# A planned eight-image kernel: quarter mask products, array halves, packed denominators, one spreading load

## Time and profile before

| what | value |
|---|---|
| median of 3 runs | 984.56 us (983.65 to 985.37) |
| span of the profiled execution, first to last instruction | 980.1 us |
| busy: PE, DVE, ACT, POOL | 875.3, 595.7, 457.1, 204.5 us |
| mean granted clock of PE | 0.962 of full speed |

### The profile page before, as it was taken

How to read it: one execution, slowest core, us unless ns; L and a number is a source line. 1 busy time by engine, 2 the same in 40 slices (tenths; PEclk the granted TensorE clock), 3 DMA queues, 4 the chain that set the end, 5 groups by cost and what they waited for, 6 DMA issues and landing times.

```text
span 980.1 us, 22296 instructions
## 1 busy us (share of the span) xinstructions
PE 875.3 (89%) x9216; PEld 588.9 (60%) x9216; DVE 595.7 (61%) x1666; ACT 457.1 (47%) x764; POOL 204.5 (21%) x274
## 2 busy tenths in 40 slices
PE   9888798999999999999999999999988879978876
PEld 8675475566666665666566566656555555644553
DVE  5545534673688468845884588558844764653456
ACT  1003326453555355525543655356435645524754
POOL 1002100120225012401341124112411231131122
PEclk9999689999999999999999999999979999998988
DMA  7100000000000000000000001000100100030000
GB/s 198 25 7 1 1 6 23 23 23 28 23 23 23 28 23 23 23 28 23 23 23 28 7 23 39 23 1 23 39 11 26 36 23 23 23 81 23 2 1 22
DMA packets 25572, 25.84 MB, mean 26 GB/s; under 512 B 14688, under 2 KB 20576, under 8 KB 25344
## 3 DMA queue, kind: packets, MB, share of 16 engines
q1 hardware_dynamic: 25472, 24.42, 8.7%
HBM read 19.69 MB, written 4.72 MB: 25 GB/s over the span
## 4 chain that ended last, share of the span: by engine, by line
PE 58%; DVE 17%; ACT 11%; issue 6%; DMA 5%; POOL 2%; SPq 1%; POOLq 0%; DVEq 0%; ACTq 0%
PE ring L934 7%; PE pv L955 5%; PE side_a L633 5%; PE ring L889 5%; PE pv L973 4%; ACT pr L1190 4%; DVE rden L1676 3%; DMA scale<-branch_scale 3%; PE heads L879 2%; PE side_a L642 2%; PE heads L914 2%; PE ring L929 2%; DMA branch_scale<-rden 2%; PE heads L861 2%; PE ring L897 2%
## 5 line engine op out<-in xcount | busy, mean ns | idle before, releaser
L1190 ACT ACTIVATE pr<-ring 128x1024 f32<-128x1024 f32 (+1 forms) x128 | 120.9, 944 | 108.3 <-PE ring L938 61.0
L934 PE MATMUL ring<-kq 64*128 64x256 f32 (+2 forms) x1280 | 136.5, 341 | 0.7 <-ACT kq L1242 0.5
L934 PEld LDWEIGHTS ring<-kq 64*128 64x128 f32 x1280 | 96.3, 191 | 42.6 <-issue 30.8
L1234 ACT ACTIVATE kq<-ring 128x896 f32<-128x896 f32 x64 | 58.8, 919 | 85.3 <-PE ring L889 85.3
L1686 DVE SCALAR_TENSOR_TENSOR ob<-pv,all_gates,scale 128x256 f32<-128x256 f32 x96 | 46.3, 482 | 85.3 <-PE pv L973 38.4
L1661 DVE TENSOR_REDUCE toks<-heads 128x2 f32<-128x512 f32 x64 | 44.3, 692 | 84.8 <-PE heads L919 83.4
L573 POOL TENSOR_TENSOR toks<-ta,tb 128x128 f32<-128x128 f32 (+1 forms) x96 | 39.7, 434 | 180.4 <-DVE tb L1652 180.4
L1242 ACT ACTIVATE kq<-ring 128x256 f32<-128x256 f32 x64 | 24.6, 384 | 107.5 <-PE ring L897 107.0
L1676 DVE RECIPROCAL rden<-pv 128x256 f32<-128x256 f32 x32 | 56.2, 1756 | 25.5 <-PE pv L955 25.0
L536 POOL TENSOR_TENSOR oT<-ob 128x256 f32<-128x256 f32 x32 | 23.3, 727 | 226.3 <-DVE ob L1686 226.3
L889 PE MATMUL ring<-early,toks 128*128 128x128 f32 x448 | 63.5, 284 | 7.5 <-ACT pr L1190 7.4
(11 more groups left out here) (377 smaller groups left out, 1704.4 us busy)
## 6 DMA issues: line engine op xcount, KB each, us to landing
scale<-branch_scale SPq DMA_DIRECT2D x128, 96.0 KB, 2.3
branch_scale<-rden SPq DMA_DIRECT2D x32, 128.0 KB, 1.7
late<-in_late SPq DMA_DIRECT2D x1, 2158.5 KB, 8.4
xin<-in_x SPq DMA_DIRECT2D x16, 64.0 KB, 2.2
pr<-in_prep SPq DMA_DIRECT2D x1, 602.0 KB, 3.8
y<-ob SPq DMA_DIRECT2D x8, 64.0 KB, 1.9
kq<-in_masks SPq DMA_DIRECT2D x1, 480.0 KB, 8.5
toks<-in_final SPq DMA_DIRECT2D x1, 434.0 KB, 4.4
```

The costliest lines, as they stand in the source:

```text
L934: m = pe.matmul(ring[:, j, at:at + nq], kq[rows, k, key0:key0 + P], kq[rows, k, Q + q_:Q + q_ + nq], start=r % 2 == 0, stop=at > P)
L1190: act.activation(out, in_, ACT.Exp, scale=SCALE).then_inc(S("exp_done"), 1)
L1234: act.activation(kq[:, k, :], flat[:, 0:WIDE], ACT.Copy).then_inc(S("turned"), 1)
```

## The change

- **Quarter masks.** The mask products run on quarters: for each head (half of the rows) and each half of the output partitions one product of a 64x64 block of the identity with 64 partitions of the table. The blocks off the diagonal need the tables with their partition halves exchanged: `crossed`, loaded by two more DMAs and cast on DVE.
- **3x3 convolution.** Each tap becomes two products of 128 columns, one per half image, on the two column halves. The sum with the input then stands in 128 partitions: two DVE additions, and one transpose instead of two.
- **Experts, q and keys/values.** `xp` is written twice side by side by DVE, so that one transpose gives `xpT` in both partition halves. The four hidden products use a half of the rows each (64 partitions) and all stand behind `logit_exp`; ScalarE waits once for all of them. Keys and values use the upper half, q the lower. Two more DMAs put the second halves of `w1` and of `q3` at partitions 64 to 127.
- **Denominators.** Row `32j + 2 br + x` holds branch `br` and token half `x`: six rows of 128 columns instead of three of 256. 32 products instead of 24, a reciprocal of 128 x 128, a store of half the bytes, and one load for all four heads.

```diff
-        onesk = sb("onesk", [P, BR, 32])
+        onesk = sb("onesk", [P, BR, 2, 32])
...
+            sp.dma_start(crossed32[0:C, :], masks_in[C:P, P:mn]).then_inc(S("masks"), 16)
+            sp.dma_start(crossed32[C:P, :], masks_in[0:C, P:mn]).then_inc(S("masks"), 16)
...
+            sp.dma_start(late[C:P, a:a + 2 * P], late_in[0:C, a:a + 2 * P]).then_inc(S("head_weights"), 16)
+            sp.dma_start(late[C:P, q:q + P], late_in[0:C, q:q + P]).then_inc(S("head_weights"), 16)
...
-                    for j in range(4):
-                        sp.dma_start(scale[32 * j:32 * j + 32, :, :], scale_out[32 * j:32 * j + BR, :].unsqueeze(0)
-                                     .broadcast_to((32, BR, T))).then_inc(S("scale_loaded"), 16)
+                    sp.dma_start(scale[:, :, :].rearrange("p b t -> p (b t)"),
+                                 scale_out.rearrange("(j r) t -> j (r t)", j=4)[:, 0:BR * T].unsqueeze(1)
+                                 .broadcast_to((4, 32, BR * T))).then_inc(S("scale_loaded"), 16)
...
                 for i, (copy, dy, dx) in enumerate(PAIRS3):
-                    m = pe.matmul(SA[0:C, 0:T], bin1[:, i, :], window(copy, dy + 1, dx + 1), start=(i == 0),
-                                  stop=(i == 4))
+                    for up in range(2):
+                        m = pe.matmul(SA[C * up:C * up + C, 0:P], bin1[:, i, :], half_window(up, copy, dy + 1, dx + 1),
+                                      start=(i == 0), stop=(i == 4))
...
-                for t in range(NT):
-                    m = pe.transpose(SA[:, t * C:(t + 1) * C], x1[0:C, t * P:(t + 1) * P], ident[0:C, 0:C])
-                m.then_inc(S("x2_turned"), 1)
+                pe.transpose(SA[:, 0:P], x1[:, 0:P], ident).then_inc(S("x2_turned"), 1)
...
-                for i in range(2):
-                    m = pe.matmul(SC[:, i * T:(i + 1) * T], w1[:, i, :], xpT[:, :], start=True, stop=True)
-                m.then_inc(S("hidden"), 1)
                 yield
                 pe.wait_ge(S("logit_exp"), image * 2 + 2)
                 for i in range(2):
-                    m = pe.matmul(SB_[:, i * T:(i + 1) * T], w1[:, 2 + i, :], xpT[:, :], start=True, stop=True)
+                    for x in range(2):
+                        rows = slice(C * x, C * x + C)
+                        m = pe.matmul((SC, SB_)[x][:, i * T:(i + 1) * T], w1[rows, 2 * x + i, :], xpT[rows, :],
+                                      start=True, stop=True)
...
-                pe.matmul(SC[:, 0:T], cst("q3"), xpT[:, :], start=True, stop=True).then_inc(S("q3_out"), 1)
-                for t in range(NT):
-                    m = pe.matmul(SB_[:, t * T:(t + 1) * T], xpT[:, t * P:(t + 1) * P], cst("kv3"),
+                for t in range(NT):
+                    m = pe.matmul(SB_[:, t * T:(t + 1) * T], xpT[0:C, t * P:(t + 1) * P], cst("kv3")[0:C, :],
                                   start=True, stop=True)
+                    if t == 0:
+                        pe.matmul(SC[:, 0:T], cst("q3")[C:P, :], xpT[C:P, :], start=True, stop=True)\
+                            .then_inc(S("q3_out"), 1)
...
-                    pe.wait_ge(S("head_weights"), 16 * 28)
+                    pe.wait_ge(S("head_weights"), 16 * 30)
...
+            def masked(banks, at, n, straight, over, first):
+
+                for j in range(2):
+                    rows = slice(C * j, C * j + C)
+                    for c in range(2):
+                        m = pe.matmul(banks[C * c:C * c + C, j, at:at + n], identb[rows, rows],
+                                      (straight if c == j else over)[rows, 0:n], start=first, stop=not first)
+                return m
...
-                    for j in range(2):
-                        pe.matmul(heads[:, j, 0:2 * P + BAND], identb, max_b, start=True, stop=False)
+                    masked(heads, 0, 2 * P + BAND, max_b, max_x, True)
...
-                    for j in range(2):
-                        m = pe.matmul(ring[:, j, 0:P], identb, score_b[:, 0:P], start=False, stop=True)
+                    m = masked(ring, 0, P, score_b, score_x, False)
...
-                pieces = [(0, 0, T, 0, 0), (0, P, T, 1, 0), (1, 0, T, 0, T),
-                          (2, P, T, 1, P), (2, P, BAND, 1, 3 * P), (2, 0, P, 1, 2 * P)]
-                for i, (br, q_, end, part, a) in enumerate(pieces):
+                pieces = [(0, 0, P, 0, 0), (0, 1, P, 0, P), (0, 1, P, 1, 0), (1, 0, P, 0, T), (1, 1, P, 0, T + P),
+                          (2, 1, P, 1, P), (2, 1, WINDOW, 1, 3 * P), (2, 0, P, 1, 2 * P)]
+                for i, (br, x, n, part, a) in enumerate(pieces):
                     for j in range(4):
-                        m = pe.matmul(PV[32 * j:32 * j + 32, T + q_:T + end], onesk[:, br, :],
-                                      prob(g, j, part, a, end - q_), start=(i == 0), stop=(i == 5))
+                        m = pe.matmul(PV[32 * j:32 * j + 32, T:T + n], onesk[:, br, x, :],
+                                      prob(g, j, part, a, n), start=(i == 0), stop=(i == 7))
...
+                act.wait_ge(S("hidden"), image + 1)
                 for u in range(2):
-                    act.wait_ge(S("hidden"), image * 2 + u + 1)
...
+                    if which in (2, 3):
+                        from_ = from_.unsqueeze(1).broadcast_to((P, 2, C))
...
-                V.tensor_tensor(x1[0:C, :], SA[0:C, 0:T], x1[0:C, :], ALU.add).then_inc(S("x2"), 1)
+                for up in range(2):
+                    rows = slice(C * up, C * up + C)
+                    a = V.tensor_tensor(x1[rows, 0:P], SA[rows, 0:P], x1[rows, up * P:up * P + P], ALU.add)
+                a.then_inc(S("x2"), 1)
...
-            dve.wait_ge(S("masks"), 16)
-            link(V.tensor_copy(masks[:, :], masks32))
+            dve.wait_ge(S("masks"), 48)
+            V.tensor_copy(masks[:, :], masks32)
+            link(V.tensor_copy(crossed[:, :], crossed32))
...
-                V.reciprocal(rden[:, :], PV[:, T:2 * T]).then_inc(S("inverted"), 1)
+                V.reciprocal(rden[:, :], PV[:, T:T + P]).then_inc(S("inverted"), 1)
```

More of the change, by code:

```diff
@@ L124, in build @@
         score_b = masks[:, P + 2 * P + BAND:P + 4 * P + 2 * BAND]
+        crossed = sb("crossed", [P, mn - P], BF16)
+        crossed32 = kq[:, :, :].rearrange("p k n -> p (k n)")[:, mn + T:2 * mn + T - P]
+        max_x, score_x = crossed[:, 0:2 * P + BAND], crossed[:, 2 * P + BAND:4 * P + 2 * BAND]
         w_sm = sb("w_sm", [P, 84])
@@ L138, in build @@
         bin1 = sb("bin1", [P, 5, C])
-        binn = sb("binn", [P, 5, C])
         bnc = sb("bnc", [P, 4])
         half = sb("half", [P, 1])
-        onesk = sb("onesk", [P, BR, 32])
+        onesk = sb("onesk", [P, BR, 2, 32])
         meank = sb("meank", [P, P])
@@ L182, in build @@
         selH = sb("selH", [P, KEEP])
-        xp = sb("xp", [P, NT, C])
+        xp = sb("xp", [P, NT, 2, C])
         xpT = sb("xpT", [P, T])
@@ L197, in build @@
         scaled_q = pr[0:C, 0, 1, 0:26 * C].rearrange("p (n c) -> p n c", n=26)
-        rden = sb("rden", [P, T])
+        rden = sb("rden", [P, P])
         scale = sb("scale", [P, BR, T])
-        scale_out = nc.dram_tensor("branch_scale", (P, T), F32, kind="Internal").ap()
+        scale_out = nc.dram_tensor("branch_scale", (P, P), F32, kind="Internal").ap()
         ob = sb("ob", [P, 2, BR, T])
@@ L209, in build @@
         hm = sb("hm", [P, 4, T])
+        binn = hm[:, :, :].rearrange("p g t -> p (g t)")[:, 0:5 * C].rearrange("p (n m) -> p n m", n=5)
         cmp_, cmq_ = keep5[:, 0:NT, :], keep5[:, NT:2 * NT, :]
@@ L449, in _ @@
             sp.dma_start(late[C:P, v:v + HEADS * VDIM], late_in[0:C, v:v + HEADS * VDIM]).then_inc(S("head_weights"), 16)
+            a, q = lo["w1"][0] + 2 * P, lo["q3"][0]
+            sp.dma_start(late[C:P, a:a + 2 * P], late_in[0:C, a:a + 2 * P]).then_inc(S("head_weights"), 16)
+            sp.dma_start(late[C:P, q:q + P], late_in[0:C, q:q + P]).then_inc(S("head_weights"), 16)
             for x in range(2):
@@ L598, in transpose_tok, with turn_twice @@
                 m.then_inc(S(done), 1)
+            def turn_twice(done):
+                pe.sem_inc(S("pe_gap"), 1)
+                for t in range(NT):
+                    m = pe.transpose(SB_[:, t * P:(t + 1) * P], xp[:, t, :, :].rearrange("p x c -> p (x c)"), ident)
+                m.then_inc(S(done), 1)
             IDLE = dict(loads=24, route1=4, route2=12,
@@ L744, in back @@
                 after(n, "xn2")
-                transpose_tok(xp, SB_, 0, "xn2_turned")
+                turn_twice("xn2_turned")
                 yield
@@ L917, in max_scores @@
                 if kind == "A":
-                    for j in range(2):
-                        m = pe.matmul(heads[:, j, P:2 * P], identb, max_b[:, 0:P], start=False, stop=True)
+                    m = masked(heads, P, P, max_b, max_x, False)
                 m.then_inc(S("max_scores"), 1)
@@ L927, in scores @@
                 else:
-                    for j in range(2):
```

(23 more changed lines are left out.)

2 lines of the change are left out of this document (1 added, 1 removed).

## The result

The change made the kernel slower: 1075.11 us median (1074.38 to 1080.62) against 984.96 before, a ratio of 1.0906 with a 95% interval of 1.0837 to 1.0975. The prediction said 944 us (926 to 968). Medians here are over all runs of a kernel, so that 984.96 holds a fourth run of 997.79 us, while the ratios leave out runs more than 1.5% above the kernel's fastest (among the experiments one run of e3 and two of e6).

The account below looks back on a forecast made before the run. PE was taken to bound the kernel, busy 89% of 980.1 us. Terms summed to 45.9 us, less 5 for first and last images and short covers: 939 us of span, 944 us median, range 926 to 968.

Parts of the forecast that it names:

- the new one lies between 2.3 and 3.8, I take 3.0: Denominators: the one load of the scale, 384 KB, was to take 3.0 us, where the old took 3.58 from last issue.
- 8.3 us become about 5.9: Denominators: reciprocal, store, issues and load of the scale together were to shorten from 8.3 us to about 5.9.
- 4.4 + 7.3: Gain from the shorter denominator chain: 4.4 us in PE's wait at L633, 7.3 at L790 together with the tail.
- PE weighs a round later, so most of it is DVE's time: Denominators: most of the shortening from 8.3 to about 5.9 us was DVE's time; PE uses the scale a round later.
- The quarters: Mask products as four 64x64 quarters at once: scores 15.0 us and maxima 9.3 saved, less 8.0 for array shape changes.
- rival 1: Mask products: quarters pair up but four do not run together, 24.3 us of the sum go, 968 us; chance 0.10.
- rival 4: Mask products: quarters run one after another, 0.72 us a group of 416 columns instead of 0.36, 1017 us; chance 0.04.
- Convolution: 3x3 convolution on column halves: 9.4 us saved over 8 images, less 1.0 for its x2 turn.
- Experts and q3: Experts' hidden products on row halves save 6.9 us; q3 running beside keys and values saves 2.6.
- Rival 2: Exp and copies, not PE, set the rounds; savings become waits before L889, L897 and L929, 962 us; chance 0.15.
- Rival 3: Mask products: every border between array shapes drains PE, 7 us more, 951 us; chance 0.12.
- PE's waits grow by more than 15 us: One of three signs named beforehand that would show the prediction wrong: PE's waits growing by over 15 us.

Follow-up runs that it names:

- e3: Changed kernel with four spreading loads, one per head, and the mask products whole again (128x128, two per group): 957.5 us, ratio 0.9709 to before.
- e6: Changed kernel with four spreading loads and the denominators as before (three rows of 256 columns a head): 977.43 us, ratio 0.9905 to before.
- e1: Changed kernel with its one spreading load cut into four, one per head, 32 partitions each: 946.84 us, ratio 0.9635 to before.
- e9: Changed kernel with four full-width loads, SP waiting for each of the first two to land before issuing the next: 1070.1 us, ratio 1.0848 to before.
- e13: Changed kernel with every denominator row given four times, so the one load reads 16 rows by 8 partitions: 947.17 us, ratio 0.9614 to before.
- e14: As e13, but one 16-row load per branch, each with its own semaphore; a branch waits for its own load alone: 942.38 us, ratio 0.9582 to before.
- e11: As e4 (three loads by branch, outermost dimension 4), but each branch waits for its own load alone: 958.55 us, ratio 0.9721 to before.
- e4: Changed kernel with the one load cut into three by branch, outermost dimension still 4, DVE waiting for all three: 1082.16 us, ratio 1.1024 to before.
- e10: Changed kernel with four stores writing each head's rows four times, and one load from 16 rows by 8 partitions: 1082.91 us, ratio 1.0971 to before.
- e2: Kernel before with only its four loads replaced by the one spreading load (three rows of 256 columns per head): 1097.52 us, ratio 1.1178 to before.

## Why the prediction was wrong

**The first step that failed** is a term: "Against it stands a load of 602 KB that landed in 3.8; the new one lies between 2.3 and 3.8, I take 3.0." It landed in 7.2 to 7.3 where the chain shows it, with a median of 6.8 over the 32 groups. The bound came from a load by bytes, and that load's outermost dimension is 128 partitions; the new one's is four. Four of 16 engines move 384 KB in 5.0 us, 16 in 2.0. By the prediction's own sum, "8.3 us become about 5.9", the chain should have shortened by 2.4 us; its median grew by 2.2, from 7.1 to 9.3. The 3.58 us that the sum took from the earlier trace rows for the old load are also a late group's: the median from the last issue to the landing is 2.3 us before, so there was less to win than 2.4.

**The second is the price of a late chain.** The prediction had counted the chain only as it gave time back, in two waits of PE and the tail (4.4 + 7.3): 11.7 us for 2.4 us of chain, some 4.9 us for each. At that price a chain 2.2 us longer would have taken the forecast from 944 to 966 us, inside its range. The step behind it, "PE weighs a round later, so most of it is DVE's time", does not hold: in 27 of the 32 groups DVE starts the first branch within 0.5 us of the landing, in the kernel before as in e1, e6, e9, e13 and after, so it stood waiting for the load nearly every time, and what PE needs stood behind it. From the start of the reciprocal to the landing, the median of the 32 groups of a trace, against the time:

| kernel | chain us | median us | clock (profiled run) |
|---|---|---|---|
| three loads, 16 rows, first third (e14) | 5.1 | 942.38 | 0.967 |
| four loads (e1) | 6.2 | 946.84 | 0.962 |
| one load, 16 rows (e13) | 6.3 | 947.17 | 0.960 |
| three loads, three waits, first third (e11) | 6.7 | 958.55 | 0.954 |
| wide denominators (e6) | 7.05 | 977.43 | 0.959 |
| before | 7.1 | 984.96 | 0.962 |
| in turn (e9) | 9.3 | 1070.1 | 0.882 |
| after | 9.3 | 1075.11 | 0.883 |
| three loads (e4) | 9.5 | 1082.16 | 0.869 |
| sixteen rows, four stores (e10) | 9.8 | 1082.91 | 0.889 |
| before with one load (e2) | 10.3 | 1097.52 | 0.907 |

From e1 to e6 a microsecond of chain goes with 35 us of time (30.6 us for 0.88), from e6 to e9 with 41 (92.7 for 2.26): about one for each of the 32 groups, and some more. The kernels differ in other things too (in e6 the reciprocal itself keeps DVE busy for 0.8 us more), so this is a trend and not a law. Below 6.2 us it may flatten: e14's first third lands 1.1 us sooner than the load of e1 and brings some 4 us, within the spread. Between 7.1 and 9.3 us the clock falls. After against e13, with the same 10312 products: PE's busy time grows by 911.0 - 844.6 = 66.4 us, the span by 128.5, so that the remaining 62.1 us are idle. The idle part goes with the hold itself, whose four waits grew from 13.4 to 76.6 us against the kernel before. The busy part goes with the clock: if it has only the levels 1.00 and 0.50, a mean of 0.883 over 1073.5 us is some 250 us at 0.50, and 0.960 over 945.0 is some 76. That split is arithmetic from the two pages: no run held the clock up while DVE was late, so what the clock alone costs wasn't isolated.

**The quarters** run as the prediction said, but save less. The four start together; the timeline of e1 (start us, us, what):

```profile
498.46 0.36 PE L924 MATMUL ring<-masks 64*64 64x416 bf16 x1
498.47 0.36 PE L924 MATMUL ring<-crossed,masks 64*64 64x416 bf16 x2
498.47 0.36 PE L924 MATMUL ring<-masks 64*64 64x416 bf16 x1
```

This excludes rival 1 (two at a time) and rival 4 (in turn), and so does the chain of e1, which answers to the earlier trace rows:

```profile
483.81 0.18 PE ring L924 x4
483.99 0.24 PE heads L924 x4
...
498.53 0.30 PE ring L924 x4
```

With 416 columns a group takes 0.24 behind quarters (0.36 before) and 0.30 behind another shape (0.46 before); with 128 columns 0.18 (0.22). The prediction had 0.19 and 0.29. So the maxima save 0.12 + 0.04 = 0.16 us a pair of groups and the scores 0.16 + 0.04 = 0.20, not 0.235, and behind another shape a group is 0.06 longer, not 0.10. The term was mis-sized: 10.9 us in place of 16.3, which these figures explain in direction but not to the microsecond.

**Convolution.** 20 products hold PE for 1.28 us in e1's timeline (469.01 to 470.29, when the next group starts), against 1.2 predicted and 2.38 before. DVE's two additions take 287 ns each in e1, 0.16 more than the one of 417 ns (0.2 predicted). The term was 8.4 and measured 6.7.

**Experts and q3** brought 5.0 of 9.5; q3 with keys and values takes 1.12 us in e1 (475.47 to 476.59) in place of 0.70 + 0.86, more than the gain predicted there, so PE's time was saved, and where the other half went, the runs don't show.

**Rival 2, the waits take it,** was right about the mechanism in one state: with the old chain (e6) the savings on PE bring 8 us of the 34 that the prediction gave them (45.9 - 11.7). Its place was wrong: the waits for the exp are as in e1 (8.0 us before the even turns in both, 7.8 and 7.3 before the odd ones), and those for DVE are longer (L807 for `m` 5.7 us against 0.6, L649 for `keep` 8.5 against 4.6). **Rival 3** can't be told from mis-sized terms.

**What the prediction named as its end** came true: "PE's waits grow by more than 15 us" (from 13.4 to 76.6 in four lines). Its other sign, "the granted clock in the middle falls below 1.00 for good", came true as a mean (0.883): the clock is 1.00 again at 522.93 to 527.94 and falls anew behind the next stall. With the engine count mended, e13 gives 947 us against the 944 that were forecast. That is in part luck: quarters, convolution and experts were put 11.6 us too high together, the denominators 19.2 too low, and the parts don't add up.

## What to carry to other kernels

Count a DMA's cost from its access pattern, not from its bytes alone: the load of 602 KB with 128 rows outermost landed in 3.8 us, the one of 384 KB with four in 7.2. A broadcast over heads or groups often makes a small outermost dimension; copies in the source rows, which cost nothing here since the product's 32 output rows were there anyway, make it wide again. And before you merge DMAs in a tightly ordered kernel, ask which engine stands in its queue until they land, and how often: here DVE did in 27 of 32 groups, and a microsecond of chain between 6.2 and 9.3 us went with 35 us of time and more. Wait for the part that is needed first.

## What the runs showed of the hardware that was not expected

- Small packets count a DMA's engines: 12832 under 512 B with one load on four, 13216 with one on sixteen (12 more for each of 32), 14752 with four on sixteen (60 more). Three loads on four engines give 13088 (e4, 8 more), three on sixteen 14240 (e14, 44 more). By the same count the four stores of e10, whose page shows 13216 as e13's does, ran on four engines each.
- Loads issued behind one another with the same outermost dimension of 4 did not spread over other engines: three at once had a share of 0.24 to 0.29 (e4).
- Around a wait of 3.0 us PE's granted clock was 1.2 GHz (0.50) through a stretch of 13.5 us, and in such stretches the same seven products took 1.49 us instead of 0.83.
- Quarters of 416 bfloat16 columns, four at once, take 0.24 us where two full products, one after the other, took 0.36: not half of it.
